# Two products of zeros after the four products of each group in the two hops

## The reference

```python
    def _L2_gnn_ref(x, edge_index):
        ...
        deg = jax.ops.segment_sum(jnp.ones_like(src, dtype=x.dtype), dst, num_segments=n)
        dinv = jax.lax.rsqrt(jnp.maximum(deg, 1.0))
        norm = (dinv[src] * dinv[dst])[:, None]
        for _ in range(K):
            x = jax.ops.segment_sum(x[src] * norm, dst, num_segments=n)
        return x
...
    x = _layernorm(x + _L0_gnn_ref(x, edge_index, edge_weight, L0_gnn_W, L0_gnn_b), axis=-1)
    x = _layernorm(x + _L1_gnn_ref(x, edge_index, L1_gnn_w, L1_gnn_fc_w, L1_gnn_fc_b, L1_gnn_bias), axis=-1)
    x = _layernorm(x + _L2_gnn_ref(x, edge_index), axis=-1)
    x = _layernorm(x + _L3_gnn_ref(x, edge_weight, edge_attr_3, edge_index, L3_gnn_w1, L3_gnn_b1, L3_gnn_w2, L3_gnn_b2), axis=-1)
```

## Time and profile before

| | us |
|---|---|
| median of 3 runs | 28398.9 |
| lowest, highest | 28390.3, 28557.1 |
| the profiled execution, its own time | 28426.8 |
| its span, first to last instruction | 28425.0 |

### The profile page before, as it was taken

One profiled execution on the slowest core, in us unless ns is written; L12 is line 12 of the kernel. 1 busy time (PEld: TensorE's weight loads), 2 busy tenths in 40 slices (PEclk: granted clock), 3 DMA queues, 4 the chain that ended last, 5 costly groups with the idle time before them and its releaser, 6 DMA issues. The chain is left out here.

```text
span 28425.0 us, 294521 instructions
## 1 busy us (share of the span) xinstructions
PE 13463.4 (47%) x65171; PEld 12839.1 (45%) x65172; DVE 11716.9 (41%) x26884; ACT 5703.5 (20%) x18021; POOL 17105.9 (60%) x17490
## 2 busy tenths in 40 slices
PE   1333333333333339995333333333333378888887
PEld 0333333333333339995333333233333367777777
DVE  1376611111111127774111111111111189999999
ACT  6411122100000002221000000000000045555554
POOL 2677766366666650002666666666666667777777
PEclk8555555555555558886555555555555578888888
DMA  1111111222222221110000000200000222222223
GB/s 45 15 15 15 15 15 15 11 58 60 59 59 60 59 54 30 30 30 17 12 12 12 12 12 12 13 11 12 12 12 12 11 48 50 50 50 50 50 50 47
DMA packets 1840282, 855.51 MB, mean 30 GB/s; under 512 B 1295919, under 2 KB 1624848, under 8 KB 1839379
## 3 DMA queue, kind: packets, MB, share of 16 engines
q0 software_dynamic: 532480, 382.75, 9.6%
q1 hardware_dynamic: 1307008, 471.30, 7.4%
q10 hardware_dynamic: 692, 0.49, 0.0%
HBM read 757.65 MB, written 96.92 MB: 30 GB/s over the span
## 5 line engine op out<-in xcount | busy, mean ns | idle before, releaser
L937 POOL DMA_INDIRECT hop_far<-hop_rows,hop_index x6656 | 6280.0, 944 | 5902.7 <-issue 4778.7
L973 PE MATMUL hop_total<-hop_far,hop_hot 128*128 128x32 f32 x13312 | 3139.6, 375 | 6368.5 <-issue 3598.0
L973 PEld LDWEIGHTS hop_total<-hop_far,hop_hot 128*128 128x128 f32 x13312 | 3090.4, 321 | 6419.1 <-issue 6416.6
L743 POOL DMA_INDIRECT weighted_far<-in_x_dram,weighted_rows x3328 | 3412.2, 1025 | 1991.1 <-issue 1033.3
L952 DVE TENSOR_TENSOR hop_hot<-hop_iota,local_of_edge 128x512 f32<-128x512 f32 x1664 | 1097.7, 688 | 8337.8 <-DMA rows_by_src<-push_row,push_index 6706.5
L1048 POOL DMA_INDIRECT rows_by_src<-push_row,push_index x3328 | 3186.2, 957 | 1689.1 <-issue 1509.3
L2059 POOL DMA_INDIRECT conv_far<-conv_rows x3328 | 3171.9, 953 | 1043.4 <-issue 814.8
L2167 PE MATMUL conv_radial_a<-radial,conv_hidden 128*128 128x256 f32 x6656 | 2890.4, 523 | 797.1 <-DVE conv_products_b L2286 616.6
L1097 PE MATMUL push_near<-far_rows_sb,push_turned 128*128 x6656 | 1687.0, 434 | 3170.2 <-DVE push_turned L1075 1683.5
L826 PE MATMUL weighted_total<-weighted_message,weighted_hot 128*128 128x33 f32 x6656 | 1566.8, 398 | 3391.8 <-issue 1727.5
L1097 PEld LDWEIGHTS push_near<-far_rows_sb,push_turned 128*128 128x128 f32 x6656 | 1600.9, 327 | 3256.3 <-issue 3254.1
(11 more groups left out here) (255 smaller groups left out, 20792.1 us busy)
## 6 DMA issues: line engine op xcount, KB each, us to landing
push_line<-local_by_group SPq DMA_DIRECT2D x832, 256.0 KB
hop_far<-hop_rows,hop_index POOLq DMA_INDIRECT x6656
conv_weights<-weight_by_group SPq DMA_DIRECT2D x832, 128.0 KB
att_far<-rows_by_src SPq DMA_DIRECT2D x880, 80.0 KB
weighted_far<-in_x_dram,weighted_rows POOLq DMA_INDIRECT x3328
rows_by_src<-push_row,push_index POOLq DMA_INDIRECT x3328
conv_far<-conv_rows POOLq DMA_INDIRECT x3328
weighted_rows<-edges_by_dst SPq DMA_DIRECT2D x1664, 8.0 KB
```

What stands on the lines that cost most here:

```text
L743: pool.indirect_dma_start(far[s][:, j, :], None, table, bass.IndirectOffsetOnAxis(ap=rows[s][:, j, 0:1].bitcast(I32), axis=0)).then_inc(ga ...
L937: pool.indirect_dma_start(far[s][:, j, :], None, table, bass.IndirectOffsetOnAxis(ap=index[s][:, j:j + 1], axis=0)).then_inc(gathered[s], 16)
L973: last = pe.matmul(total[:].rearrange("p n c -> p (n c)")[:, bass.ds(at[s * HALVES + j // COLUMNS] * F, F)], hot[s][:, j, :], far[s][:, j, ...
```

## The change

After the four products of a group, and after the one that raises `added[s]`, TensorE makes two more: zeros (128x128) as weights, zeros (128x384) as moving data, added to the first 384 columns of PSUM bank 0 and of bank 1 of `hop_total`. They wait for nothing, raise no semaphore, and read only the tile `zeros` that `open_sums` and `close_sums` use.

```diff
+IDLE = 384
...
@@ hop_sum, TensorE @@
                                          hot[s][:, j, :], far[s][:, j, :], start=False, stop=False)
                     last.then_inc(added[s], 1)
+                    for n in range(2):
+                        pe.matmul(total[:, n, 0:IDLE], zeros[:, 0:P], zeros[:, 0:IDLE], start=False, stop=False)
             close_sums(pe, total, zeros, closed)
```

## The result

| | before | changed |
|---|---|---|
| median, 20 runs each | 28474.4 us | 28700.2 us |
| lowest, highest | 28376.7, 28588.8 | 28524.9, 28726.8 |
| the profiled execution | 28426.8 | 28541.2 |

The ratio is **1.0055, with a 95% interval of 1.0033 to 1.0077**. The forecast was 27300 us. One thing is needed to read single runs: those of either kernel fall on two levels about 170 us apart (28390 and 28570 before, 28540 and 28714 after), because the attention stage, which the change leaves alone, takes 2475 us at a granted clock of 0.94 (the profiled execution of the changed kernel) or 2655 at 0.85 (that of the kernel before). Level by level the change costs about 150 us.

The account below looks back on a forecast made before the run. GpSimd's gathers were taken to set the hops' pace, held up by TensorE's late signals: 28426.8 - 1123 (lateness) + 5 (later `close_sums`) = 27309 us, stated as 27300. Range 27250 to 29000 us.

Parts of the forecast that it names:

- Step 1, the cost of the zeros: Hops, TensorE: zeros take 2.56 or 1.28 us a group, fit within the 4.996 us between groups, 0 us on the path.
- Step 2, who waits behind them: Hops: ScalarE and VectorE don't wait for the zeros; only `close_sums` starts later at each hop's end, +5 us in all.
- the 5 us: Added time for two hops, because `close_sums` starts up to 2.56 us later at the end of each.
- Step 3, the clock: Hops: the zeros raise TensorE's clock well above 0.50 on average, which by itself gives 0 us.
- Step 4, the signals: Hops: with TensorE busy, its late signals to ScalarE's copies vanish, taking away all 1123 us; the trace couldn't price it.
- the 1123 us: Excess of both hops' long gather stretches over GpSimd's undisturbed pace, 1103 us of it waits for ScalarE's copies; forecast as removable.
- The one that gave the lateness to the gathers: Rival, hops: unbroken gathering holds TensorE's signals back, so nothing TensorE does matters; 28432 us, chance 0.17.
- The slower rival: Hops: signals stay late and the zeros' extra instructions make them later; 28994 us, chance 0.28.
- its 1.40 us each: Slower rival's fixed time per TensorE instruction in late stretches: 22.4 us for a group of 16, 33.6 us for 24.
- A queue filled by the number of instructions: Support for the slower rival: 24 instructions a group fill TensorE's queue of 64 in 2.7 groups instead of 4.
- The floor: Hops: GpSimd's gathers alone, never waiting, take 4.996 us a group, reached if all 1123 us go.
- a result within 1%: Whole kernel: time changes by less than 1% (284 us), the case of the gathers, chance 0.17.

Follow-up runs that it names:

- e8: The changed kernel plus a break of GpSimd (clearing a 128x256 scratch tile and waiting) after each group: 28956.4 us, ratio 1.0188 to the kernel before.
- e15: The changed kernel itself, run again on a second chip without late signals: 26183.3 us, kernel before there 26165.1 us.
- e7: The changed kernel with zeros of 128 columns instead of 384: 28707.5 us, ratio 1.0085 to the kernel before.
- e2: The kernel before plus a GpSimd break (clearing a 128x256 scratch tile and waiting) after each group: 29030.9 us, beside 28554.2.
- e17: The kernel before with only the first of a group's four products, on a chip with late signals: 28169.5 us, beside 28591.7.
- e10: The changed kernel with six products of zeros of 128 columns instead of two of 384: 25995.4 us, kernel before there 26159.3.
- e14: The same kernel as e10, on a second chip without late signals: 26165.3 us, kernel before there 26165.1.
- e9: The kernel before with only the first of a group's four products, on a chip without late signals: 25981.5 us, kernel before there 26159.3.
- e13: The same kernel as e9, on a second chip without late signals: 25984.2 us, kernel before there 26165.1.
- e1: The kernel before with SyncE issuing four plain transfers a group in place of GpSimd's indirect gathers in both hops: 22068.6 us, beside 28554.2.
- e11: The kernel before gathering 16 floats a row instead of 32, on a chip without late signals: 26101.1 us, kernel before there 26159.3.
- e12: The kernel before with three gathers a group instead of four, on a chip without late signals: 23894.1 us, kernel before there 26159.3.
- e16: The same kernel as e12, on a second chip without late signals: 23891.3 us, kernel before there 26165.1.
- e5: The kernel before plus the GpSimd break of e2 after every second group: 28523.5 us, ratio 1.0024.
- e6: The kernel before plus the GpSimd break of e2 after every fourth group: 28590.3 us, ratio 1.0011.
- e3: The kernel before with products added to fixed columns instead of those a register names: 28532.2 us, beside 28554.2.
- e4: The kernel before with VectorE reading `iota` from SBUF instead of PSUM: 28368.5 us, beside 28554.2.

## Why the prediction was wrong

- **Step 1, the cost of the zeros: right in its part.** They start 0.32 us apart at the full clock, fit between the gathers, and 0 us lies on the path as TensorE's work. e8 and e15 show it directly (0 us a hop). What it did not count was that an instruction could cost in another currency: 10.3 ns of the common budget, 8 x 10.3 ns x 1664 groups = 137 us of the 150 measured.
- **Step 2, who waits behind them: right.** Nobody was found waiting for a product of zeros on the path, and the 5 us can't be told.
- **Step 3, the clock: right.** 0.50 to 0.64, worth 0 us; e7, without the rise, costs the same.
- **Step 4, the signals: wrong, and it was the whole forecast.** "I take all of it, since the nearest rows of a busy TensorE, the convolution's, show no late signal at all." None of the 1123 us went: GpSimd's waits for the copies grew from 1124 to 1331 us, with the clock at 0.64 and TensorE busy 57% of a hop. The convolution gathers a group in 6.6 us, slower than the 5.9 at which e2's hops were free of late signals. The stages also differed in GpSimd's pace, which stands in the same windows (3790 GpSimd instructions in 5000 us, about 760 of them not gathers), and the text itself called it a correlation over stages that differ in other things. e2 separated them: clock 0.50, idle TensorE, 5.9 us a group, nothing late.
- **The rivals.** The one that gave the lateness to the gathers (28432 us, chance 0.17) had the cause and the better number. Its evidence, that signals come after GpSimd has stopped, was only a hint; e2 made it more. Its "nothing that TensorE does matters" is off by 150 us. The slower rival had the sign and the unit, instructions and not columns; its 1.40 us each was the length of a stall divided by what happened to be in it. Measured over the hop it is 10 ns. A queue filled by the number of instructions isn't borne out as the cause of the loss: with 4 instructions a group e17 loses 487 us a hop all the same.
- **The floor was real.** 4.99 to 5.00 us a group runs over whole hops on the two chips without late signals, with zeros (e10, e14, e15) and without (e9, e13). It is nothing that this edit could reach.
- **The range** of 27250 to 29000 held the result because it was wide enough for the rivals, not because the forecast was near; the chance given to a result within 1% was 0.17.

Left open: what the shared thing is. Three of the five chips that the batches of experiments fell on have it short and two have not, and nothing in the kernel decides it. Another small sign divides them alike: the page gives a time from issue to landing for the gathers in e15 ("x6656, 2.4") and in all other runs on the two chips, and in none on the three. Behind this lie records that are missing. Each gather raises its semaphore by 16 as it lands, 53248 times a hop (as each plain transfer does in e1), and of these events the trace of the first hop holds 9077 in the kernel before, 12240 in the changed one and 4952 in e17, but 48336 in e2, 53184 in e1 and 52816 in e15. In the hops lateness and missing records come and go together. The convolution, which is not slowed, loses some too (51581 events before, 89011 in e15). So a rival stands that no run tests: that the recording of the events is itself what is short, or part of it. All runs here were recorded, and none shows how long the hops take, or whether signals are late, without it. Half the bytes (e11) and fewer gathers (e12, e16) are untried where signals are late.

## What to carry to other kernels

Before you explain a wait by an engine's clock or idleness, look at what every other engine does while the wait lasts, and measure from the last event that the wait needs to the moment when it ends, for every group and not for one. An engine that falls silent before the stall ends is a suspect and no more, for it may be silent because it waits too. A correlation over stages is settled by one cheap run that changes only one of the two, here a break of 0.9 us. Filling an idle engine with work is not free if it shares something with the bound: price it by instructions, and expect the price to be there on some chips and not on others.

## What the runs showed of the hardware

- The same kernel takes 28399 to 28604 us on three chips and 26159 and 26165 us on two, 8% less. All of it lies in the four stages that gather faster than a group in 6.6 us. All executions were recorded ones.
- On the slower ones a group of four gathers of 128 rows and TensorE's 16 instructions has a budget of about 5.7 us in a hop, where GpSimd alone would need 5.0. Breaks of GpSimd count towards it one for one (1094 and 1120 us of breaks and waits in e5 and e6, 1124 of waits alone before). On these chips, with 16 instructions or more and gathers by GpSimd, signals were in time at 5.9 us a group (e2, e8) and late at 5.7 (e5, e6).
- Where signals are late, the copy that waits for TensorE's completion signal starts up to 41 us after the start of the last product (41.0 before, 39.9 changed, over both hops), and the product starts spread to 2.8 us, with the clock raised to 0.64 as at 0.50. Where they are not, it is never more than 0.54 us (e1, e2, e8, e9 to e16).
- With plain transfers issued by SyncE in place of indirect gathers the hops' signals are never late, at 1.8 us a group, on a chip where they are late with the gathers (e1 beside e3 and e4).
